# A graph kernel of four layers: x1 transposed by transfers, v in other PSUM banks, the sums' products moved

## The reference

```
x1 = LN(x  + normalise((adj @ x + x) @ W0 + b0))
A  = exp(8 tanh(x1 Wq Wk' x1' / (8 sqrt(128)))) * adj, divided by its row sums
x2 = LN(x1 + A @ x1 @ V)
x3 = LN(x2 + ((si + sj' + wr*adj + gb) @ x2) @ W2 + b2)     si = x2 . w_i, sj = x2 . w_j
x4 = LN(x3 + relu(sum over k of T_k(L) @ x3 @ W3_k + b3))   L = I - D^-1/2 adj D^-1/2, three Chebyshev terms
```

## Time and profile before

| | |
|---|---|
| median of 3 runs | 675.4 us (673.63 to 675.59) |
| profiled execution, its own time | 675.26 us |
| its span, first to last instruction | 673.2 us |
| mean granted TensorE clock | 0.989 |
| PE busy | 630.7 us, 94% |
| DVE busy | 588.1 us, 87% |
| ACT busy | 417.9 us, 62% |

### The profile page before, as it was taken

How to read it: one execution, slowest core, us unless ns; L and a number is a source line. 1 busy time by engine, 2 the same in 40 slices (tenths; PEclk the granted TensorE clock), 3 DMA queues, 4 the chain that set the end, 5 groups by cost and what they waited for, 6 DMA issues and landing times.

```text
span 673.2 us, 17817 instructions
## 1 busy us (share of the span) xinstructions
PE 630.7 (94%) x7574; PEld 482.4 (72%) x7574; DVE 588.1 (87%) x1529; ACT 417.9 (62%) x723; POOL 73.5 (11%) x50
## 2 busy tenths in 40 slices
PE   8896779989999999999999999999999999799894
PEld 4454545779667986789667986789767986449794
DVE  7989899789899899889899899889898889899435
ACT  6969797254883659365883659465883659424402
POOL 0101210011001200021001200021001200111002
PEclk9999989989999999999999999999999999989998
DMA  8610000001000100002000100002000100000102
GB/s 339 242 64 1 1 1 1 1 2 33 2 1 1 45 22 2 1 2 64 1 2 1 39 28 1 2 1 65 1 2 2 33 2 1 1 1 2 33 2 64
DMA packets 12447, 18.76 MB, mean 28 GB/s; under 512 B 592, under 2 KB 9040, under 8 KB 12368
## 3 DMA queue, kind: packets, MB, share of 16 engines
q1 hardware_dynamic: 12368, 17.63, 7.8%
HBM read 13.44 MB, written 4.19 MB: 26 GB/s over the span
## 4 chain that ended last, share of the span: by engine, by line
PE 65%; DVE 25%; ACT 5%; issue 2%; POOL 1%; ACTq 0%; DVEq 0%
PE r L1304 13%; PE r L1306 13%; PE r L1305 13%; DVE p_lo L896 4%; DVE att L891 4%; PE r L1352 4%; PE av L1462 3%; DVE stats L580 3%; PE av L1465 2%; PE av L1464 2%; ACT att L399 2%; PE m L1304 2%; PE m L1306 2%; PE m L1305 2%; PE r L1310 2%
## 5 line engine op out<-in xcount | busy, mean ns | idle before, releaser
L246 POOL TENSOR_TENSOR small<-small,minus_half 128x8 f32<-128x8 f32 (+1 forms) x40 | 69.1, 1732 | 587.8 <-DVE small L607 295.7
L891 DVE TENSOR_TENSOR att<-att,adjT 128x1024 f32<-128x1024 f32 x64 | 77.9, 1218 | 7.2 <-ACT att L401 7.1
L399 ACT ACTIVATE att<-r,coef 128x1024 f32<-128x1024 f32 x64 | 70.4, 1100 | 16.3 <-PE r L1306 15.8
L896 DVE SCALAR_TENSOR_TENSOR p_lo<-p_hi,att 128x1024 f16<-128x1024 f16 x64 | 77.8, 1217 | 0.0
L1304 PE MATMUL r<-xq,a_hi 128*128 128x128 f16 x448 | 76.0, 219 | 0.0
L1306 PE MATMUL r<-xq,a_lo 128*128 128x128 f16 x448 | 76.0, 219 | 0.0
L1305 PE MATMUL r<-xq,a_hi 128*128 128x128 f16 x448 | 76.0, 219 | 0.0
L1304 PE MATMUL r<-rs,a_hi 128*128 128x128 f16 x448 | 75.8, 219 | 0.0
L1306 PE MATMUL r<-rs,a_lo 128*128 128x128 f16 x448 | 75.8, 219 | 0.0
L1305 PE MATMUL r<-rs,a_hi 128*128 128x128 f16 x448 | 75.8, 219 | 0.0
L289 ACT ACTIVATE p_hi<-att 128x1024 f16<-128x1024 f32 x64 | 66.8, 1044 | 5.8 <-DVE att L891 5.7
(11 more groups left out here) (402 smaller groups left out, 2124.3 us busy)
## 6 DMA issues: line engine op xcount, KB each, us to landing
adjT<-in_adj_t SPq DMA_DIRECT2D x8, 512.0 KB, 7.9
x<-in_x SPq DMA_DIRECT2D x7, 512.0 KB, 5.0
out<-outb SPq DMA_DIRECT2D x7, 512.0 KB, 3.5
pq<-in_adj SPq DMA_DIRECT2D x2, 512.0 KB, 8.5
u<-in_adj SPq DMA_DIRECT2D x2, 512.0 KB, 9.2
tmp<-in_adj SPq DMA_DIRECT2D x2, 512.0 KB, 9.7
x2s<-in_adj SPq DMA_DIRECT2D x2, 512.0 KB, 9.4
outb<-in_x SPq DMA_DIRECT2D x1, 512.0 KB, 11.2
```

What stands on the lines that cost most here:

```text
L246: return nc.gpsimd.tensor_tensor(dst, src, minus_half[:, 0:src.shape[-1]], ALU.pow)
L399: nc.scalar.activation(att[:, s], dst[:], ACT.Tanh, scale=c_tanh).then_inc(S["th"], 1)
L891: tt(att[:, s], att[:, s], adjT[:, t, :], ALU.mult).then_inc(S["pm"], 1)
L896: stt(p_lo[:, s], p_hi[:, s], -LO_UP, att[:, s], ALU.mult, ALU.add).then_inc(S["pl"], 1)
```

## The change

For batches 2 to 7, x1 is no longer transposed on PE. ACT writes the high part of x1 in row form to a new buffer `x1r` (`x1_row_hi`), DVE the low part (`x1_row_lo`), and SP transposes each part by a transfer from SBUF to SBUF (`transpose=True`, 256 KB each) into `xts`. `g_product` waits for both transfers. SP's queue has each batch's load of x, its store and then the two transfers.

v goes to the third bank of `av` and to m7 instead of r1. So `scores(i, 0)`, which writes r1, waits for g alone, and the wait for `v_lo` stands behind `scores(i, 1)`. On PE the last laplacian piece is split: its first three chunks (36 products) come ahead of `g_product`, the fourth (12 products) between g and v. `sums_w2` moves from ahead of `next_scores(i, 3)` to behind it. On DVE three `sj` steps stand together, and the second `end_sum` comes ahead of `v_lo`.

```diff
+        x1r = sb("x1r", [P, 2, N], F16)
@@ sync
-            for i in range(2, B):
-                if i < B - 1:
-                    sp.wait_ge(S["e0"], i + 1)
-                    sp.dma_start(x0[:], x[i + 1]).then_inc(S["x_in"], 16)
-                sp.wait_ge(S["ln3_a"], i - 1)
-                sp.dma_start(out_v[i - 2], outb[:]).then_inc(S["stored"], 16)
+            for i in range(1, B - 1):
+                if i + 2 < B:
+                    sp.wait_ge(S["e0"], i + 2)
+                    sp.dma_start(x0[:], x[i + 2]).then_inc(S["x_in"], 16)
+                if i >= 2:
+                    sp.wait_ge(S["ln3_a"], i - 1)
+                    sp.dma_start(out_v[i - 2], outb[:]).then_inc(S["stored"], 16)
+                for part, name in enumerate(("hi", "lo")):
+                    sp.wait_ge(S[f"x1r_{name}"], i)
+                    sp.dma_start(cd(xts[(i + 1) % 2][:, part]), x1r[:, part], transpose=True).then_inc(S[f"x1d_{name}"], 16)
+            sp.wait_ge(S["ln3_a"], B - 2)
+            sp.dma_start(out_v[B - 3], outb[:]).then_inc(S["stored"], 16)
@@ scalar
+            def x1_row_hi(b):
+                act.wait_ge(S["ln0_v"], b + 1)
+                act.wait_ge(S["ln0_a"], b + 1)
+                if b > 2:
+                    act.wait_ge(S["x1d_hi"], 16 * (b - 2))
+                copy(cd(x1r[:, 0]), xas[b % 2][:], X_UP).then_inc(S["x1r_hi"], 1)
@@ scalar, back
-                x1t_hi(i + 1, r1)
+                x1_row_hi(i + 1)
                 g_hi(i + 1, r2)
-                v_hi(i + 1, r1)
+                v_hi(i + 1, (av[:, 2], m7))
@@ vector
+            def x1_row_lo(b):
+                if b > 2:
+                    dve.wait_ge(S["x1d_lo"], 16 * (b - 2))
+                dve.wait_ge(S["x1r_hi"], b - 1)
+                stt(cd(x1r[:, 1]), xas[b % 2][:], X_UP, cd(x1r[:, 0]), ALU.mult, ALU.subtract).then_inc(S["x1r_lo"], 1)
@@ vector, back
                 q_lo(z_all, i - 1, 1)
-                for k_ in range(2):
+                x1_row_lo(i + 1)
+                for k_ in range(3):
                     sj_step(sj_ch, i, k_)
-                x1t_lo(i + 1, r1)
-                sj_step(sj_ch, i, 2)
                 end_sum(i - 1, 0)
                 g_lo(i + 1, r2)
-                v_lo(i + 1, r1)
+                end_sum(i - 1, 1)
+                v_lo(i + 1, (av[:, 2], m7))
                 if i + 2 < B:
                     x0_max(i + 2)
-                end_sum(i - 1, 1)
                 sj_step(sj_ch, i, 3)
@@ tensor
             def g_product(b, dst):
                 xt = xts[b % 2]
+                if b >= 2:
+                    pe.wait_ge(S["x1d_hi"], 16 * (b - 1))
+                    pe.wait_ge(S["x1d_lo"], 16 * (b - 1))
                 for h in range(2):
-                    pe.wait_ge(S["x1t_lo"], 2 * b + h + 1)
+                    if b < 2:
+                        pe.wait_ge(S["x1t_lo"], 2 * b + h + 1)
@@ tensor, scores
                 for h in range(2):
+                    if i >= 2 and t == 0:
+                        pe.wait_ge(S["g_lo"], 2 * i + h + 1)
@@ tensor, front
-                pe.wait_ge(S["v_lo"], 2 * (i + 1))
                 scores(i, 0)
                 pe.wait_ge(S["fa"], 2 * (i - 1))
                 scores(i, 1)
+                pe.wait_ge(S["v_lo"], 2 * (i + 1))
                 if nxt:
                     pe.wait_ge(S["y2_lo"], 2 * (i - 1))
                     row_max_sum(i + 1)
...
                 next_scores(i, 2)
+                next_scores(i, 3)
                 if nxt:
                     pe.wait_ge(S["x_st"], 5 * (i + 1) + 1)
                 sums_w2(m7, i - 1)
-                next_scores(i, 3)
@@ tensor, back
                 laplacian_part(r0, xq, 1, 0, C // 2)
-                x1_t(i + 1, r1)
                 pe.wait_ge(S["q_lo"], 2 * i)
                 laplacian_part(r0, xq, 0, C // 2, C).then_inc(S["o_mm"], 1)
+                laplacian_part(r0, xq, 1, C // 2, 7)
                 pe.wait_ge(S["u_ok"], i)
                 g_product(i + 1, r2)
-                v_product(i + 1, r1)
-                laplacian_part(r0, xq, 1, C // 2, C).then_inc(S["o_mm"], 1)
+                laplacian_part(r0, xq, 1, 7, C).then_inc(S["o_mm"], 1)
+                v_product(i + 1, (av[:, 2], m7))
```

More of the change, by code:

```diff
@@ L157, in cd, with chunks4 @@
             return ap.rearrange("p (c d) -> p c d", c=C)
+        def chunks4(ap):
+            return ap.rearrange("p (c d) -> p c d", d=D)
         z_all = Stage(x3, xq, rs, pq, u, outb, r0)
@@ L382, in g_hi, with v_hi @@
                     copy(gs[b % 2][:, 0, half(h)], src[:, half(h)], W_DOWN).then_inc(S["g_hi"], 1)
-            def v_hi(b, src):
+            def v_hi(b, srcs):
                 for h in range(2):
                     act.wait_ge(S["v_mm"], 2 * b + h + 1)
-                    copy(vhis[b % 2][:, half_chunks(h), 0:D], cd(src[:])[:, half_chunks(h)], W_DOWN).then_inc(S["v_hi"], 1)
+                    copy(vhis[b % 2][:, half_chunks(h), 0:D], chunks4(srcs[h][:]), W_DOWN).then_inc(S["v_hi"], 1)
             def v_scaled(b):
@@ L435, in start @@
                 y0_hi(1, 1, av[:, 2])
-                v_hi(0, r1)
+                v_hi(0, (r1[:, half(0)], r1[:, half(1)]))
                 for t in range(C):
@@ L449, in start @@
                 g_hi(1, r1)
-                v_hi(1, r0)
+                v_hi(1, (r0[:, half(0)], r0[:, half(1)]))
                 for t in range(C):
@@ L907, in g_lo, with v_lo @@
                     split_lo(gs[b % 2][:, 1, half(h)], src[:, half(h)], W_DOWN, gs[b % 2][:, 0, half(h)], "g", 2 * b + h + 1)
-            def v_lo(b, src):
+            def v_lo(b, srcs):
                 for h in range(2):
                     hc = half_chunks(h)
-                    split_lo(vlos[b % 2][:, hc], cd(src[:])[:, hc], W_DOWN, vhis[b % 2][:, hc, 0:D], "v", 2 * b + h + 1)
+                    split_lo(vlos[b % 2][:, hc], chunks4(srcs[h][:]), W_DOWN, vhis[b % 2][:, hc, 0:D], "v", 2 * b + h + 1)
             class Rows:
@@ L987, in start @@
                 y0_lo(1, 1, av[:, 2])
-                v_lo(0, r1)
+                v_lo(0, (r1[:, half(0)], r1[:, half(1)]))
                 gate_weights(wj_ch)
@@ L1017, in start @@
                 row_scales()
-                v_lo(1, r0)
+                v_lo(1, (r0[:, half(0)], r0[:, half(1)]))
                 row_sums(0)
@@ L1433, in g_product, with v_product @@
                 xt = xts[b % 2]
+                if b >= 2:
+                    pe.wait_ge(S["x1d_hi"], 16 * (b - 1))
+                    pe.wait_ge(S["x1d_lo"], 16 * (b - 1))
                 for h in range(2):
-                    pe.wait_ge(S["x1t_lo"], 2 * b + h + 1)
+                    if b < 2:
+                        pe.wait_ge(S["x1t_lo"], 2 * b + h + 1)
                     split_product(dst[:, half(h)], ms[:, 0], ms[:, 1], xt[:, 0, half(h)], xt[:, 1, half(h)],
                                   True, True).then_inc(S["g_mm"], 1)
-            def v_product(b, dst):
+            def v_product(b, dsts):
                 for h in range(2):
-                    project_half(dst, xts[b % 2], vs[:, 0], vs[:, 1], h).then_inc(S["v_mm"], 1)
+                    for j in range(C // 2):
+                        c = h * C // 2 + j
+                        l_ = split_product(dsts[h][:, chunk(j)], xts[b % 2][:, 0, chunk(c)], xts[b % 2][:, 1, chunk(c)],
+                                           vs[:, 0], vs[:, 1], True, True)
+                    l_.then_inc(S["v_mm"], 1)
             def scores(i, t):
@@ L1484, in start @@
                 adj_x0(1, 6, C, av[:, 2], 0, False)
-                v_product(0, r1)
+                v_product(0, (r1[:, half(0)], r1[:, half(1)]))
                 pe.wait_ge(S["g_lo"], 2)
@@ L1506, in start @@
                 attend(0, 6)
-                v_product(1, r0)
+                v_product(1, (r0[:, half(0)], r0[:, half(1)]))
                 pe.wait_ge(S["g_lo"], 4)
```

## The result

| | before | after |
|---|---|---|
| device us, median (range, runs) | 675.5 (673.6 to 676.9, 4) | 682.7 (681.1 to 683.1, 4) |
| profiled execution: its time, its span | 675.26, 673.2 | 682.82, 680.7 |
| PE, DVE, ACT busy us | 630.7, 588.1, 417.9 | 628.9, 590.7, 418.7 |
| one pass of the loop, steady | 75.9 | 76.5 |

The ratio is 1.0103 [1.0076, 1.0129]: slower by about 1%, 7.2 us. The forecast was 684.3, slower. PE's work is a little shorter and the kernel longer, so the time lies in waits. The windows over one pass of the changed kernel, with columns as in the earlier trace rows, say the same: PE is idle for most of 1 us in 76.5, the clock is 1.00.

The account below looks back on a forecast made before the run. PE was taken to bound the kernel (75.95 of 76 us busy in a pass), with DVE at 92% next. The order's 4.5 us and the transfers' 4.5 us made +9.0, so 684.3 us from 675.4; range 671 to 704.

Parts of the forecast that it names:

- order, five passes: Sums' products behind scores 3, net of the removed transposes: 0.85 us lost in each of five passes.
- late transfers: Transposing transfers ahead of g_product: landing 4.25 us after issue, 0.75 us late in each of six passes, 4.5 us.
- Step 1: Transposes leave PE (0.87 us); the piece behind them then waits for q_lo and starts at 390.70: gain 0.61 us.
- Step 2: Row copies on ACT (1.06 us) and DVE (1.22 us): no gain, but high ready at 390.6, low at 391.9.
- Step 3: When g_product can start: PE ready at 395.41, transfers landing in 4.25 us (bounds 3.5 and 14.7), 0.75 us late.
- T: The time g_product can start: 395.41 if the transfers have landed, 0.75 us later by the forecast landing.
- Rival B: Transfers go block by block, up to 14.7 us a part, g_product 24.6 us late: 828 us; chance 0.06.
- Step 4: From g_product to scores: scores 0 at 398.7, first tanh at 400.6, DVE's sums at 402.7 as before.
- Step 5: sums_w2 behind scores 3: PE idles 0.65 us, l2_read not before 405.9, attend(i, 0) at 409.3, PE waits 1.0 us.
- A: Transfers land over 5.5 us, PE idles each pass and its clock may drop: 692.4 to 707 us; chance 0.17.
- C: Faster: the front swallows the late l2_read and transfers land in 3.5 us: 671.6 or 669.4 us; chance 0.18.
- D: No change: transfers hidden, about half of the sums' move absorbed, within 2 us of 675.4; chance 0.12.

Follow-up runs that it names:

- shifted_code: sums_back with 64 products of 8 columns in place of 7 keep-busy ones at PE's start, moving its later code: 675.6 us, ratio 0.9990.
- sums_back: The changed kernel with the sums' products (sums_w2) ahead of scores 3 again: 674.9 us, ratio 0.9994.
- before_sums_moved: The kernel before with only the sums' products (sums_w2) moved behind scores 3: 681.1 us, ratio 1.0077.
- sig_late: sums_back with DVE's row maximum step earlier and its fourth sj step moved behind sums(i - 1) in front: 680.9 us, ratio 1.0085.
- no_transfers: The changed kernel without the two transposing transfers and the waits for them, leaving out x1's transposition for batches 2 to 7: 680.2 us, ratio 1.0056.
- sums_back_pe_transposes: sums_back with x1 transposed on PE again: 677.8 us, ratio 1.0040.

## Why the prediction was right

Side and size were right, and so was the larger mechanism, the order. Late transfers there were, but not the even delay of every pass that the sum has. Both large terms were sized too high, and that the total came within 1.6 us is in part luck: the 1.4 us at the end, which no step had, stand in for part of what these overrated.

| term | predicted us | profile of after |
|---|---|---|
| order, five passes | 4.25 | 3.14 |
| order, last front | 0.3 | 0.33 |
| late transfers | 4.5 (six of 0.75) | 2.60 (0.99, 1.53 and 0.08) |
| end | 0 | 1.42 |
| sum | 9.0 | 7.5 (medians: 7.2) |

*Step 1.* The piece restarts at 390.62 on before's scale (predicted 390.70): 0.18 us of wait for `q_lo` in place of 0.87 of transposes. Right.

*Step 2.* ACT's row copy takes 1.06 us and DVE's 1.23, as taken from the earlier trace rows. Right.

*Step 3.* The failed size. I took 4.25 us to landing, the middle between the plain rows of 3.5 and 5.0. The median is 3.2. It is the row of the plain store (3.5) that was near, and T is 395.32, when PE's own work allows it: the delay was nothing in four passes (0.08 us in one of them). The other two were late for a reason that I hadn't named, and that no mean delay describes: each has an instruction fetch at the transfer (shifted_code). The rule that I weighed, the Trainium skill's "Advanced Engine Details and Errata", section "X-Bar Transpose (TRN2)", as fast as plain transfers, fits the median landing: 3.2 us for 256 KB beside 3.9 and 4.5 for plain ones of 512 KB. By it my sum would have been 4.5 us smaller, 679.8, short of the result, as it doesn't cover the two late ones. The same section expects 350 to 400 GB/s; here the two parts, 0.52 MB, stream in about 2.9 us (394.9 to 397.7), some 180 GB/s, and most slices of that window show 170 to 240. Rival B is out: eight blocks landed in 3.2 us. The 1309 ns that the Trainium skill's "VectorE: DVE Perf Modes", section "The three transpose paths", gives for one block can't be multiplied: an estimate by it for eight in a row would be 10.5 us.

*Step 4.* Scores 0 at 398.63 (398.7), first tanh at 400.42 (400.6), `sums_read` at 402.70 (402.7). Right.

*Step 5.* `l2_read` at 405.61 (405.9) behind a wait, `attend(i, 0)` at 409.02 (409.3), 1.0 us of PE lost, the waits at the fifth and sixth attends swallowed. The gap ahead of scores 3 is 0.34 us, not 0.65, which is most of why a steady pass costs 0.58 and not 0.85. One thing I hadn't seen: of the 1.0 us PE waits 0.74 already at `adj_x2(0)`, which overwrites the bank m7 that `l2_read` reads, and 0.27 at the attend. The sum is the same, since both hang on `l2_read`. That this move is the cause is shown by undoing it (sums_back) and by doing it alone (before_sums_moved), and sig_late reaches the same wait from the other side.

*The end.* No step had the 1.4 us. Two kernels without transposes on PE had the stretch early and five late, so I leave open what sets its place, and whether the 1.4 us are in the medians.

*Rivals.* A: no landing over 5.3 us, and the clock stayed 1.00 behind both waits; out. B: out. C decided by whether `l2_read` comes by about 404.7: it comes at 405.61, so C fell; in sums_back, where it follows mask 0 at once, a pass is 75.60, 0.3 less than before, not the 0.61 and more that C gave: PE now waits 0.20 us for `x0_max` and 0.34 us for `xb`. D: the transfers weren't hidden twice, and of the 0.85 us a pass of the order 0.58 stayed, not half; out.

Left open: why the first pass loses 0.25 us more than the others (`no_transfers` has it too: 76.73 us), and how the 0.37 us that sums_back_pe_transposes loses divides among v's banks, the split piece, DVE's `end_sum` and SP's order; neither was tried.

## What to carry to other kernels

A small product has the price of whoever reads it: ask who reads the result, what stands behind that reader in its own queue, and which bank it frees. Here two products, 0.45 us together, moved behind 1.3 us of others, cost 0.9 us a pass and all that the transfers had saved. Where two engines are near their bound, fill a wait with work that has no reader soon, and order products so that the operand that comes by transfer is needed last, which covered 1.7 of the 2.5 us of its long landings here.

## What the hardware showed that I had not expected

- Two transposing transfers of 256 KB (float16, 1056 packets each), SBUF to SBUF, 1.3 us apart, land 3.1 to 3.2 us after their issues; their issue takes SP's queue 1.24 to 1.43 us each, where a plain one took 0.58.
- Where an instruction fetch of 16 KB falls to them, their stream stands still for 1.05 to 1.25 us, beginning 0.6 to 1.0 us after the fetch does: landings of 4.1 to 5.3 us in place of 3.2 (the longest with an 8 KB fetch besides), at other batches when code was shifted. Whether plain transfers are held up alike isn't shown.
- Half a MB a pass moved within SBUF costs PE, DVE and ACT nothing that can be seen (a pass of 76.49 us with and without it).
